# Norm and plain attention between two routed layers as one stage by groups of four tiles, and the experts' output bias split on 128 partitions

## The chip, the cores and the metric

The kernel runs on one core of a Trainium2 chip. The metric is the time of one execution in microseconds (us), the median of several runs. A core has TensorE (PE), VectorE (DVE), ScalarE (ACT), GpSimd (POOL) and SyncE (SP), which here only issues DMAs; they run side by side and wait for each other by semaphores.

## The reference

The program is a decoder of four layers over x (2 x 1024 tokens, width 256, fp32), with 77 context rows per batch element. Each layer is an attention and a feed-forward on the normed x. What this case touches:

```python
def _L2_xattn_ref(q, k, v, mask):          # q: layer norm of x; k = v = the 77 context rows
    scale = jnp.asarray(D_MODEL, q.dtype) ** (-0.5)
    logits = jnp.einsum('bqd,bkd->bqk', q, k) * scale
    logits = logits + mask.astype(q.dtype) * NEG_BIG
    weights = jax.nn.softmax(logits, axis=-1)
    return jnp.einsum('bqk,bkd->bqd', weights, v)
...
    # the feed-forward of layers 1 and 2: eight experts, with biases
    h = jax.nn.relu(jnp.einsum('td,edh->eth', x_flat, W1) + b1[:, None, :])
    expert_out = jnp.einsum('eth,ehd->etd', h, W2) + b2[:, None, :]
...
    x = x + _L1_ffn_ref(_layernorm(x, axis=-1), ...)                       # routed, two experts a token
    x = x + _L2_xattn_ref(_layernorm(x, axis=-1), ctx_1024, ctx_1024, mask_Bx1xS2_ik0)
    x = x + _L2_ffn_ref(_layernorm(x, axis=-1), ...)                       # routed by a threshold
```

Around them stand layer 0's attention and quantised feed-forward, layer 1's attention with 16 heads and self-attention with its own projections, and layer 3's attention and routed feed-forward.

## The kernel before

x lies in SBUF as 16 tiles of 128 tokens (`core.x`, in the profile `x_resid`), its norm as `x_norm`, the norm turned (width on the partitions) as `x_normT`. The program is a row of stages. In a stage each engine has its own list of instructions, in written order; at its end all engines meet, and the next stage begins on all of them. Inside a stage they wait by semaphores. All weight loads and stores go through SP's one queue, in order.

The routed layer m1 (`routed_layer`) ends by adding its rows to x in DRAM; SP then reloads x by four DMAs, a group of four tiles each. Then come:

- **the norm** (`layer_norm`, lines 136 to 222): DVE takes statistics of all 16 tiles (L177), moments (L180), adds eps (L182); ACT takes the root of all (L205), DVE its reciprocal (L184) and the 16 normed tiles (L187). PE turns four tiles at a time (L220), ACT and DVE copy one half each from PSUM to `x_normT` (L168).
- **plain attention** (`plain_cross_attention`, from L1265): PE makes the scores of all 16 tiles, two calls a tile (L1308; an fp32 call is two passes in the trace). DVE adds the mask (L1359), takes the maximum (L1362) and subtracts it (L1363) for eight tiles at a time, ACT takes the exponentials tile by tile, with their sums (L1330). When all 16 are there, PE turns them (L1316), ACT copies them (L1333), and PE multiplies by the context rows (L1324). Of each group three tiles are weighed on ACT (`shares`, L1341) and added to x on POOL (L1302), the fourth is weighed and added on DVE (L1382). DVE takes the new x's statistics and moments (L1373, L1377) and SP stores x by groups (L74).
- **the routed layer m2**, whose first steps are POOL's reciprocal roots of the moments (L1795, L1797) and DVE's normed tiles (L1982); SP fetches expert weights (L1767, L1768).

The output bias b2 of the experts (8 x 256, fp32) is added by PE in a routed tile's last matmul (L1927): it is split into three bf16 parts, on partitions 0, 32 and 64 of a tile of 65, and multiplied by `route.pick`, which is 1 on those three rows and 0 on the others. The split (`split_output_bias`, L342 to L351) is five POOL instructions over 2048 columns. For m2 it stands in the plain attention, ahead of POOL's additions to x. For m1 it stands in the self-attention, ahead of POOL's additions of `bo` (L2487).

The self-attention has a stage of projections before it (`self_attention`, first stage). There each of 16 steps makes three bf16 parts of a projection in turn on ACT (L2299, L2308) and DVE (L2344, L2352), and SP stores them by three DMAs (L2257); ACT's first part of step n waits for the stores of step n - 2, and its second part of step n - 1 comes behind it in ACT's list.

## Time and profile before

| what | value |
|---|---|
| median of 3 runs | 2260.05 us (2259.99 to 2260.06) |
| the profiled execution's own time | 2263.76 us |
| its span | 2262.0 us |
| mean granted clock of TensorE | 0.93 |
| norm stage, in the span | 1315.86 to 1331.00 us |
| plain attention's stage | 1331.00 to 1361.64 us |

The span is the time from the first to the last instruction of the profiled execution; times in the rows are from its start. "Busy" is time in which an engine ran an instruction; "idle before" is an engine's idle time ahead of it, with the engine and line that ended it. The granted clock is 1.00 for 2.4 GHz and 0.50 for 1.2 GHz. DVE instructions that follow each other overlap a little in the rows, so that the distance of their starts is busy time over their count.

### The profile page before, as it was taken

The numbers are of one execution on the slowest core, as the hardware profiler recorded it, in microseconds if no ns is written. First come the engines' busy times: TensorE is split into PE (matmuls) and PEld (weight loads), VectorE is DVE, ScalarE is ACT, GpSimd is POOL, SyncE is SP. The second block draws the span as 40 slices with busy tenths as digits, with TensorE's granted clock in tenths as the row PEclk, the third lists the DMA queues.
The fourth block names the chain that finished last, engine by engine and source line by source line (L and its number), as shares of the span: only waits on it lengthen the run. The fifth ranks groups of instructions, "written<-read, shape, count | busy, mean of one in ns | idle before, by whom it ended". The sixth has DMA issues, their size and how long they took to land. (4 is left out here: it accounts for less than half of the span.)

```text
span 2262.0 us, 39043 instructions
## 1 busy us (share of the span) xinstructions
PE 1963.4 (87%) x12250; PEld 1425.4 (63%) x12254; DVE 1058.9 (47%) x2418; ACT 911.7 (40%) x1930; POOL 758.7 (34%) x806
## 2 busy tenths in 40 slices
PE   6699989854999999849999945999999998696897
PEld 5466656522223232339999844999999997464797
DVE  6785844624877787263233245222222221486221
ACT  2322642123777777713333321333333333264132
POOL 0123963403000000043444332343443433584343
PEclk9699999976999999969999976999999999798899
DMA  4003300023111111083222129222222221205611
GB/s 160 20 1 135 113 1 1 18 81 104 37 37 49 42 37 37 2 302 104 35 32 36 29 62 357 48 35 33 36 34 35 35 33 26 69 20 185 198 34 24
DMA packets 124544, 151.27 MB, mean 67 GB/s; under 512 B 27210, under 2 KB 104875, under 8 KB 124315
## 3 DMA queue, kind: packets, MB, share of 16 engines
q1 hardware_dynamic: 93677, 117.61, 16.2%
q0 software_dynamic: 24288, 31.81, 8.7%
q10 hardware_dynamic: 6480, 0.59, 0.3%
q8 instruction: 55, 0.90, 0.2%
q14 instruction: 44, 0.36, 0.1%
HBM read 114.35 MB, written 37.36 MB: 67 GB/s over the span
## 5 line engine op out<-in xcount | busy, mean ns | idle before, releaser
L1915 PE MATMUL banks<-m_rowsT,x_normT 128*128 128x128 f32 x4032 | 481.1, 278 | 11.8 <-issue 7.6
L1915 PEld LDWEIGHTS banks<-m_rowsT,x_normT 128*128 128x128 f32 x4032 | 470.4, 195 | 29.2 <-issue 11.8
L1924 PE MATMUL banks<-m_w,m_hT 128*128 x2016 | 462.9, 383 | 7.3 <-ACT m_hT L2150 5.6
L1924 PEld LDWEIGHTS banks<-m_w,m_hT 128*128 128x128 f32 x2016 | 376.4, 192 | 57.1 <-issue 8.5
L2160 ACT ACTIVATE m_y<-banks,m_weight 128x256 f32<-128x256 f32 x126 | 59.7, 474 | 633.5 <-PE banks L1927 528.3
L2592 ACT ACTIVATE sh_pT<-banks 128x1024 f32<-128x1024 f32 x256 | 250.7, 1024 | 26.0 <-PE banks L2551 26.0
L2150 ACT ACTIVATE m_hT<-banks,m_bias 128x128 f32<-128x128 f32 x848 | 230.3, 387 | 64.5 <-PE banks L1915 60.3
L1834 POOL DMA_INDIRECT scratch_acc<-m_y,m_row_ids x106 | 169.7, 1601 | 130.8 <-ACT m_y L2160 88.5
L2616 DVE TENSOR_REDUCE sh_mhalf<-banks 128x1 f32<-128x512 f32 x308 | 194.1, 683 | 35.2 <-PE banks L2500 35.2
L2084 DVE TENSOR_SCALAR x_normT<-m_w 128x2048 f32 x129 | 158.4, 1228 | 74.7 <-issue 71.0
L1820 POOL COPY m_row_ids<-m_ids 128x1 int32 x117 | 52.0, 444 | 330.0 <-DMA scratch_acc<-m_y,m_row_ids 211.2
L2551 PE MATMUL banks<-sh_qs,sh_ks 99*128 99x512 bf16 x512 | 151.9, 381 | 10.2 <-ACT sh_pT L2592 8.0
L1823 POOL DMA_INDIRECT m_rows<-scratch_rows,m_row_ids x117 | 126.3, 1080 | 100.4 <-POOL m_row_ids L1820 98.7
L2500 PE MATMUL banks<-sh_ks,sh_qs 96*128 96x512 bf16 x410 | 135.2, 385 | 0.0
L2087 DVE TENSOR_SCALAR m_bias<-m2p_b 128x8 f32 x69 | 14.6, 212 | 255.0 <-ACT m_hT L2150 142.6
L2541 PE MATMUL banks<-sh_pT,sa_vh 128*17 128x512 f32 x1024 | 132.0, 597 | 1.2 <-ACT sh_pT L2592 1.2
L2487 POOL TENSOR_TENSOR x_norm<-x_norm,sp_bo 128x256 f32<-128x256 f32 x16 | 11.6, 726 | 338.5 <-DVE sh_m L2626 338.5
L2099 DVE COPY m_rowsT<-banks 128x256 f32<-128x256 f32 x88 | 37.4, 425 | 179.2 <-PE banks L1906 174.1
L2551 PEld LDWEIGHTS banks<-sh_qs,sh_ks 99*128 99x128 bf16 x512 | 41.1, 97 | 116.1 <-ACT sh_pT L2592 51.5
L2621 DVE CUSTOM_DVE_ANT_0 sh_rise<-banks,sh_rise 128x512 f32<-128x512 f32 x102 | 68.6, 688 | 44.2 <-ACT sh_rise L2580 43.9
L2500 PEld LDWEIGHTS banks<-sh_ks,sh_qs 96*128 96x128 bf16 x410 | 40.0, 98 | 76.8 <-DVE sh_mhalf L2616 35.9
L2580 ACT ACTIVATE sh_rise<-banks 128x512 f32<-128x512 f32 x102 | 60.2, 598 | 63.9 <-PE banks L2500 61.1
(401 smaller groups left out, 2724.9 us busy)
## 6 DMA issues: line engine op xcount, KB each, us to landing
m_w<-L_W SPq DMA_DIRECT2D x32, 1024.0 KB, 10.5
m_w<-L1f_W SPq DMA_DIRECT2D x16, 1024.0 KB, 10.1
a_bt<-bias SPq DMA_DIRECT2D x16, 616.0 KB, 3.8
scratch_parts<-sp_part SPq DMA_DIRECT2D x48, 128.0 KB, 1.9
sh_ks<-scratch_parts SPq DMA_DIRECT2D x96, 64.0 KB, 2.2
scratch_rows<-x_norm SPq DMA_DIRECT2D x12, 512.0 KB, 9.7
sh_qs<-scratch_parts SPq DMA_DIRECT2D x90, 64.0 KB, 2.3
scratch_acc<-x_resid SPq DMA_DIRECT2D x8, 512.0 KB, 3.1
```

Source lines behind the costliest of these rows:

```text
L1823: pool.indirect_dma_start(rows[:, v, :], None, table, bass.IndirectOffsetOnAxis(ap=row_ids[:, v:v + 1], axis=0), bounds_check=TOK, oob_is_ ...
L1834: pool.indirect_dma_start(stream, bass.IndirectOffsetOnAxis(ap=row_ids[:, v:v + 1], axis=0), y[:, v, :], None, bounds_check=TOK - 1, oob_i ...
L1915: mm = pe.matmul(ps[:, H_BANK[u] + f // 4, f % 4 * P:(f % 4 + 1) * P], w1_tile[:, u, k, f * P:(f + 1) * P], rowsT[:, u, k, :], start=(k == ...
L1924: mm = pe.matmul(ps[:, Y_BANK[u], 0:D], hT[:, u, f, :], w2_sb[:, bass.ds(e, 1), f, :], start=(f == 0), stop=(f == FB - 1 and not biased))
L2084: ins = dve.tensor_scalar(w1_tile[:, u, :, :], w1_sb[:, bass.ds(e, 1), :, :].rearrange("p e k f -> p (e k) f"), 0.0, None, ALU.add)
L2150: ins = act.activation(hT[:, u, f, :], ps[:, H_BANK[u] + c, j * P:(j + 1) * P], func, bias=bias[:, u, f:f + 1])
L2500: pe.matmul(ps[:, bank["a", s, c], :], qs[u][0:SR, h, t * P:(t + 1) * P], keys, start=True, stop=True).then_inc(a_mm, 1)
L2541: mm = pe.matmul(ps[32 * g:32 * g + DK + 1, O_BANK, :], vh[:, b * KT + k, head, :], pT[:, (2 * k + h) % 4, half, :], start=(k == 0), stop= ...
L2551: mm = pe.matmul(ps[:, B_BANK + 2 * (n % 2) + half, :], ks[u][:, h, k * P:(k + 1) * P], qs[u][:, h, half * CH:(half + 1) * CH], start=True ...
L2592: act.activation(pT[:, n % 4, :, :], ps[:, B_BANK + 2 * (n % 2):B_BANK + 2 * (n % 2) + 2, :], ACT.Exp, scale=DK ** -0.5).then_inc(exp_done, 1)
L2616: dve.tensor_reduce(mhalf[:, s % 2, half, col:col + 1], ps[:, bank["a", s, c], :], AX, ALU.max).then_inc(a_max, 1)
L2621: dve.tensor_tensor_reduce(more, ps[:, bank["a", s, c], :], more, 1.0, -3e38, ALU.add, ALU.max, mhalf[:, s % 2, 0, col:col + 1]).then_inc( ...
```

## The change

Three things change.

1. The norm and the plain attention are one stage. Each engine's list is written by groups of four tiles, with the groups overlapped by hand: while one group is at its scores, the next is normed. The reciprocal root is on POOL (a power of -0.5 for four tiles) instead of ACT and DVE. Both halves of `x_normT` are copied on ACT. The maximum isn't subtracted by DVE any more: its negative is the bias of ACT's exponential. Context rows and mask are fetched in the stage's first instructions, as before in the norm's.
2. The bias b2 is loaded as 128 partitions x 16 values, split into three parts there, stored to a scratch in DRAM and loaded back as 3 partitions x 2048. The routed matmul contracts three rows with a tile of ones. `route.pick` and its four memsets are gone.
3. The split for m1 moves from the self-attention's second stage to the projection stage before it, with its store behind step 6 and its load behind step 10 in SP's queue.

```diff
+            place("b2", [P, EXPERTS * D // P])
+            sb = lambda n, shape, dt: ctx.enter_context(core.nc.sbuf_tensor(f"{name}_{n}", shape, dt))
+            self.split, self.b2_parts = sb("b2_split", [P, 3, EXPERTS * D // P], BF16), sb("b2_parts", [3, EXPERTS * D], BF16)
+            self.turned = core.nc.dram_tensor(f"scratch_{name}_b2", (3, EXPERTS * D), BF16).ap()
...
-            fetch(sp, "b2", bcast(self.b2_from.rearrange("e d -> (e d)"), 65))
+            fetch(sp, "b2", self.b2_from.rearrange("e (q n) -> (e q) n", n=EXPERTS * D // P))
...
-        rest, parts = self.loads["b2"], self.b2_parts
+        rest, parts = self.loads["b2"], self.split
         self.loads.wait(pool)
-        pool.tensor_copy(parts[:], rest[:]).then_inc(split, 1)
-        pool.wait_ge(split, 1)
-        pool.tensor_tensor(rest[:], rest[:], parts[:], ALU.subtract).then_inc(split, 1)
-        pool.wait_ge(split, 2)
-        pool.tensor_copy(parts[0:33], rest[0:33]).then_inc(split, 1)
-        pool.wait_ge(split, 3)
-        pool.tensor_tensor(rest[0:1], rest[0:1], parts[0:1], ALU.subtract).then_inc(split, 1)
-        pool.wait_ge(split, 4)
-        pool.tensor_copy(parts[0:1], rest[0:1]).then_inc(split, 1)
-        pool.wait_ge(split, 5)
+        for i in range(3):
+            pool.tensor_copy(parts[:, i, :], rest[:]).then_inc(split, 1)
+            pool.wait_ge(split, 2 * i + 1)
+            if i < 2:
+                pool.tensor_tensor(rest[:], rest[:], parts[:, i, :], ALU.subtract).then_inc(split, 1)
+                pool.wait_ge(split, 2 * i + 2)
+    def store_parts(self, sp, split, moved):
+        sp.wait_ge(split, 5)
+        sp.dma_start(self.turned.rearrange("i (p n) -> p i n", p=P), self.split[:]).then_inc(moved, 16)
+    def load_parts(self, sp, moved):
+        sp.wait_ge(moved, 16)
+        sp.dma_start(self.b2_parts[:], self.turned).then_inc(moved, 16)
...
+            inputs.fetch(sp)
             params.fetch(sp)
-            inputs.wait(sp)
+            params.store_parts(sp, b2_split, b2_moved)
+            params.load_parts(sp, b2_moved)
...
+            for g in range(NCH):
+                own = slice(4 * g, 4 * g + 4)
+                pool.wait_ge(moments_done, 4 * g + 4)
+                pool.tensor_scalar(rstd[:, own], moments[:, own, 1], EPS, None, ALU.add).then_inc(eps_done, 1)
+                pool.wait_ge(eps_done, g + 1)
+                pool.tensor_tensor(rstd[:, own], rstd[:, own], half[:].broadcast_to([P, 4]), ALU.pow).then_inc(rstd_done, 1)
             params.split_output_bias(pool, b2_split)
...
+            def turn_tokens(g):
+                pe.wait_ge(normed, 4 * g + 4)
+                if g:
+                    pe.wait_ge(xT_sb, KD * g)
                 for k in range(KD):
-                    mm = pe.matmul(ps[:, t // PER, (t % PER) * KEYS:(t % PER + 1) * KEYS], core.xnT[:, k, t * P:(t + 1) * P],
-                                   core.ctxT[:, k, (t // 8) * KEYS:(t // 8 + 1) * KEYS], start=(k == 0), stop=(k == KD - 1))
-                if t % PER == PER - 1:
-                    mm.then_inc(s_mm, 1)
+                    for j in range(4):
+                        mm = pe.transpose(ps[:, T_BANKS[k], j * P:(j + 1) * P], xn[:, 4 * g + j, k * P:(k + 1) * P], core.ident[:])
+                    mm.then_inc(xT_mm, 1)
+            def scores(g):
+                pe.wait_ge(xT_sb, KD * g + KD)
+                if g:
+                    pe.wait_ge(s_ready, g)
+                for t in range(4 * g, 4 * g + 4):
+                    for k in range(KD):
+                        mm = pe.matmul(ps[:, S_BANK, t % 4 * KEYS:(t % 4 + 1) * KEYS], xnT[:, k, t * P:(t + 1) * P],
+                                       core.ctxT[:, k, t // 8 * KEYS:(t // 8 + 1) * KEYS], start=(k == 0), stop=(k == KD - 1))
+                mm.then_inc(s_mm, 1)
+            def turn_shares(g):
+                pe.wait_ge(exp_done, 4 * g + 4)
+                if g:
+                    pe.wait_ge(pT_sb, g)
+                for j in range(4):
+                    mm = pe.transpose(ps[0:KEYS, P_BANK, j * P:(j + 1) * P], p[:, 4 * g + j, :], core.ident[:])
+                mm.then_inc(pT_mm, 1)
+            def values(g):
+                pe.wait_ge(pT_sb, g + 1)
+                for j in range(4):
+                    t = 4 * g + j
+                    if g and j == 3:
+                        pe.wait_ge(y_sb, g)
+                    elif g:
+                        pe.wait_ge(share_sb, 3 * g - 2 + j)
+                    pe.matmul(ps[:, Y_BANKS[j], 0:D], pT[:, t, :], ctx_sb[:, t // 8, :], start=True, stop=True).then_inc(y_mm, 1)
+            turn_tokens(0)
+            scores(0)
+            turn_tokens(1)
+            scores(1)
+            turn_shares(0)
+            turn_tokens(2)
             inputs.wait(pe)
-            pe.wait_ge(exp_done, NT)
-            for g in range(NT // 4):
-                for j in range(4):
-                    mm = pe.transpose(ps[0:KEYS, 4 + g, j * P:(j + 1) * P], p[:, 4 * g + j, :], core.ident[:])
-                mm.then_inc(pT_mm, 1)
-            for t in range(NT):
-                pe.wait_ge(pT_sb, t // 4 + 1)
-                if t >= 4 and t % 4 == 3:
-                    pe.wait_ge(y_sb, t // 4)
-                elif t >= 4:
-                    pe.wait_ge(share_sb, 3 * (t // 4) - 2 + t % 4)
-                pe.matmul(ps[:, t % 4, 0:D], pT[:, t, :], ctx_sb[:, t // 8, :], start=True, stop=True).then_inc(y_mm, 1)
+            values(0)
+            scores(2)
+            turn_shares(1)
+            turn_tokens(3)
+            values(1)
+            scores(3)
+            turn_shares(2)
+            values(2)
+            turn_shares(3)
+            values(3)
...
+            def tokens_turned(g):
+                for k in range(KD):
+                    act.wait_ge(xT_mm, KD * g + k + 1)
+                    act.copy(xnT[:, k, g * CH:(g + 1) * CH], ps[:, T_BANKS[k], :]).then_inc(xT_sb, 1)
+            def exponentials(g):
+                act.wait_ge(below_done, g + 1)
+                for t in range(4 * g, 4 * g + 4):
+                    act.activation(p[:, t, :], s[:, t, :], ACT.Exp, bias=below[:, t:t + 1], accum_out=sums[:, t:t + 1]).then_inc(exp_done, 1)
+            def shares_turned(g):
                 act.wait_ge(pT_mm, g + 1)
-                act.copy(pT[:, 4 * g:4 * g + 4, :], ps[0:KEYS, 4 + g, :].rearrange("p (t n) -> p t n", n=P)).then_inc(pT_sb, 1)
-            act.wait_ge(rs_done, 1)
-            for g in range(NCH):
+                act.copy(pT[:, 4 * g:4 * g + 4, :], ps[0:KEYS, P_BANK, :].rearrange("p (t n) -> p t n", n=P)).then_inc(pT_sb, 1)
...
+            act.activation(warm[:], half[:], ACT.Exp)
+            tokens_turned(0)
+            tokens_turned(1)
+            exponentials(0)
+            tokens_turned(2)
+            shares_turned(0)
+            exponentials(1)
+            tokens_turned(3)
+            weighted(0)
+            shares_turned(1)
+            exponentials(2)
+            weighted(1)
+            shares_turned(2)
+            exponentials(3)
+            weighted(2)
+            shares_turned(3)
+            weighted(3)
...
+            def statistics(g):
+                dve.wait_ge(core.reloaded[g], 16 * core.reloads)
+                for t in range(4 * g, 4 * g + 4):
+                    dve.bn_stats(stats[:, t, :], x[:, t, :]).then_inc(stats_done, 1)
+                for t in range(4 * g, 4 * g + 4):
+                    dve.wait_ge(stats_done, t + 1)
+                    dve.bn_aggr(moments[:, t, :], stats[:, t, :]).then_inc(moments_done, 1)
+            def normed_tokens(g):
+                dve.wait_ge(rstd_done, g + 1)
+                for t in range(4 * g, 4 * g + 4):
+                    dve.tensor_scalar(xn[:, t, :], x[:, t, :], moments[:, t, 0:1], rstd[:, t:t + 1], ALU.subtract, ALU.mult).then_inc(normed, 1)
+            def limits(g):
+                own = slice(4 * g, 4 * g + 4)
+                dve.wait_ge(s_mm, g + 1)
+                dve.scalar_tensor_tensor(s[:, own, :], ps[:, S_BANK, 0:4 * KEYS].rearrange("p (t k) -> p t k", k=KEYS), D ** -0.5,
+                                         mf[:, g // 2, :].unsqueeze(1).broadcast_to([P, 4, KEYS]), ALU.mult, ALU.add).then_inc(s_ready, 1)
+                dve.wait_ge(s_ready, g + 1)
+                dve.tensor_reduce(mx[:, own], s[:, own, :], AX, ALU.max).then_inc(max_done, 1)
+                dve.wait_ge(max_done, g + 1)
+                dve.tensor_scalar(below[:, own], mx[:, own], -1.0, None, ALU.mult).then_inc(below_done, 1)
+            def reciprocals(g):
+                own = slice(4 * g, 4 * g + 4)
+                dve.wait_ge(exp_done, 4 * g + 4)
+                dve.reciprocal(rs[:, own], sums[:, own]).then_inc(rs_done, 1)
...
+            statistics(0)
+            statistics(1)
+            normed_tokens(0)
+            statistics(2)
+            normed_tokens(1)
+            statistics(3)
+            inputs.wait(dve)
+            dve.tensor_scalar(mf[:], mi[:], NEG, None, ALU.mult).then_inc(masked, 1)
+            dve.wait_ge(masked, 1)
+            limits(0)
+            normed_tokens(2)
+            limits(1)
+            reciprocals(0)
+            normed_tokens(3)
+            limits(2)
+            reciprocals(1)
+            outputs(0)
+            limits(3)
+            reciprocals(2)
+            outputs(1)
+            reciprocals(3)
+            outputs(2)
+            outputs(3)
...
-                    mm = pe.matmul(ps[:, Y_BANK[u], 0:D], route.pick[:], params.b2_parts[:].rearrange("p (e d) -> p e d", e=EXPERTS)[:, bass.ds(e, 1), :],
+                    mm = pe.matmul(ps[:, Y_BANK[u], 0:D], route.ones[0:3], params.b2_parts[:].rearrange("p (e d) -> p e d", e=EXPERTS)[:, bass.ds(e, 1), :],
...
+                    if n == 6:
+                        params.store_parts(sp, b2_split, b2_moved)
+                    if n == 10:
+                        params.load_parts(sp, b2_moved)
...
+                params.split_output_bias(pool, b2_split)
...
-                params.split_output_bias(pool, b2_split)
...
-                layer_norm(core, "n8", x, xn, xnT, arrivals=core.reloaded, fetch=inputs.fetch)
```

In the merged stage VectorE's list differs most. Before, in the norm and at the start of the attention (`n_` names the norm's tiles, `a_` the attention's, `banks` is PSUM):

```order
L177 BN_STATS n_stats<-x_resid 128x6 x16
L180 BN_AGGR n_moments<-n_stats 128x2 x16
L182 TENSOR_SCALAR n_moments<-n_moments 128x16
L184 RECIPROCAL n_rstd<-n_std 128x16
L187 TENSOR_SCALAR x_norm<-x_resid,n_moments,n_rstd 128x256 x16
L168 COPY x_normT<-banks 128x512 x4
```

And now, up to the scores of the first group:

```order
L1422 BN_STATS stats<-x_resid 128x6 x4
L1425 BN_AGGR moments<-stats 128x2 x4
L1422 BN_STATS stats<-x_resid 128x6 x4
L1425 BN_AGGR moments<-stats 128x2 x4
L1430 TENSOR_SCALAR x_norm<-x_resid,moments,rstd 128x256 x4
L1422 BN_STATS stats<-x_resid 128x6 x4
L1425 BN_AGGR moments<-stats 128x2 x4
L1430 TENSOR_SCALAR x_norm<-x_resid,moments,rstd 128x256 x4
L1422 BN_STATS stats<-x_resid 128x6 x4
L1425 BN_AGGR moments<-stats 128x2 x4
L1475 TENSOR_SCALAR a_mf<-a_mask 128x154
L1435 SCALAR_TENSOR_TENSOR a_s<-banks,a_mf 128x308
```

The first group is normed after eight tiles' statistics instead of 16, and statistics of later groups stand between; DVE copies no half of `x_normT`.

TensorE, before, in both stages:

```order
L220 MATMUL banks<-ident,x_norm 128x128 x32
L139 UNCONDITIONAL_BRANCH
L1304 UNCONDITIONAL_BRANCH
L1308 MATMUL banks<-ctxT_sb,x_normT 128x77 x32
L1316 MATMUL banks<-ident,a_p 77x128 x16
L1324 MATMUL banks<-a_ctx,a_pT 128x256 x16
```

and now:

```order
L1325 MATMUL banks<-ident,x_norm 128x128 x8
L1334 MATMUL banks<-ctxT_sb,x_normT 128x77 x8
L1325 MATMUL banks<-ident,x_norm 128x128 x8
L1334 MATMUL banks<-ctxT_sb,x_normT 128x77 x8
L1343 MATMUL banks<-ident,a_p 77x128 x4
L1325 MATMUL banks<-ident,x_norm 128x128 x8
L1354 MATMUL banks<-a_ctx,a_pT 128x256 x4
L1334 MATMUL banks<-ctxT_sb,x_normT 128x77 x8
L1343 MATMUL banks<-ident,a_p 77x128 x4
L1325 MATMUL banks<-ident,x_norm 128x128 x8
L1354 MATMUL banks<-a_ctx,a_pT 128x256 x4
L1334 MATMUL banks<-ctxT_sb,x_normT 128x77 x8
```

The groups' transposes, scores, transposed exponentials and values are interleaved: values of group 0 stand ahead of the scores of group 2, so that PE, which takes its list in order, waits there for ACT's copy of the exponentials.

SyncE in the projection stage, from the last load of m1's parameters (`m_b_split` is the split of b2, `scratch_parts` the stored parts), before:

```order
L127 DMA m_b_rest<-L1f_b 65x2048
L2257 DMA scratch_parts<-sp_part 128x512 x36
L2251 DMA scratch_key_steps<-sp_part_d 128x512 x3
L2257 DMA scratch_parts<-sp_part 128x512 x6
L2251 DMA scratch_key_steps<-sp_part_d 128x512 x3
```

and now:

```order
L127 DMA m1p_b<-L1f_b 128x16
L2360 DMA scratch_parts<-sp_part 128x512 x21
L348 DMA scratch_m_b<-m_b_split 128x3x16
L2360 DMA scratch_parts<-sp_part 128x512 x12
L353 DMA m_b_parts<-scratch_m_b 3x2048
L2360 DMA scratch_parts<-sp_part 128x512 x3
```

The two rows with `scratch_m_b` are new; they stand between the stores of `sp_part`, and the load of b2 is 128x16 instead of 65x2048.

## Rows read from the trace of the kernel before

**Rows 1.** Table by stage, 1315.86 to 1331.0 and 1331.0 to 1361.64, its sum.

```profile
sum 45.78, PE 24.19 PEld 21.85 DVE 31.62 ACT 17.14 POOL 22.60; mean PE 12.10 PEld 10.92 DVE 15.81 ACT 8.57 POOL 11.30
```

**Rows 2.** Timeline, norm stage: start, us, engine, line, operation, count, idle before.

```profile
1315.91 5.32 DVE L177 BATCH_NORM_STATS2 n_stats<-x_resid 128x6 f32<-128x256 f32 x16 [23.56 <-PEq L1663]
...
1321.16 1.15 DVE L180 BATCH_NORM_AGGREGATE n_moments<-n_stats 128x2 f32<-128x6 f32 x16
...
1323.09 5.26 DVE L187 TENSOR_SCALAR x_norm<-x_resid,n_moments,n_rstd 128x256 f32<-128x256 f32 x16
...
1324.52 5.12 PE L220 MATMUL banks<-ident,x_norm 128*128 128x128 f32 x32 [19.48 <-DVE x_norm L187]
```

**Rows 3.** List of waits, both stages: sum in us, times, longest.

```profile
ACT a_p L1330 <- DVE a_s L1363: 9.8, 2, 5.3
...
PE banks L1316 <- ACT a_p L1330: 8.0, 1, 8.0
```

**Rows 4.** Timeline, attention stage, DVE and POOL.

```profile
1336.79 0.80 DVE L1363 TENSOR_TENSOR a_s<-a_s,a_mx 128x616 f32<-128x616 f32 x1
...
1339.43 4.05 POOL L344 TENSOR_TENSOR m_b_rest<-m_b_rest,m_b_parts 65x2048 f32<-65x2048 f32 x1
...
1340.29 3.85 DVE L1363 TENSOR_TENSOR a_s<-a_s,a_mx 128x616 f32<-128x616 f32 x1
```

**Rows 5.** Groups of the attention stage: busy, mean ns, idle before.

```profile
L1302 POOL TENSOR_TENSOR x_resid<-x_resid,a_shares 128x256 f32<-128x256 f32 x12 | 8.3, 735 | 0.1
...
L1341 ACT ACTIVATE a_shares<-banks,a_rs 128x256 f32<-128x256 f32 x12 | 5.5, 474 | 2.0 <-PE banks L1324 1.9
...
L1330 ACT ACTIVATE a_p<-a_s 128x77 f32<-128x77 f32 x16 | 4.0, 253 | 9.8 <-DVE a_s L1363 9.8
...
L1359 DVE SCALAR_TENSOR_TENSOR a_s<-banks,a_mf 128x308 f32<-128x308 f32 x4 | 1.9, 479 | 4.5 <-PE banks L1308 4.5
```

**Rows 6.** Timeline, start of the routed stage that follows.

```profile
1361.64 0.37 SPq L1767 DMA_DIRECT2D m_w<-L_W  x1
...
1362.02 0.24 POOL L1795 TENSOR_SCALAR rstd<-moments 128x4 f32<-128x4 f32 x1 [1.72 <-POOLq L1268]
...
1362.34 1.05 POOL L1797 TENSOR_TENSOR rstd<-rstd,minus_half 128x4 f32<-128x4 f32 x1
```

**Rows 7.** Table by stretch, PE alone: us, busy (count), granted clock, DMA.

```profile
1324.50:1327.40 2.90, 2.88 (x14) 0.50 0.00 0
...
1327.40:1328.77 1.37, 1.37 (x14) 0.98 0.00 0
...
1331.00:1338.40 7.40, 7.34 (x64) 1.00 0.35 79
...
1346.40:1349.90 3.50, 3.48 (x17) 0.50 0.00 0
...
1351.20:1355.40 4.20, 4.20 (x20) 0.98 0.08 22
```

**Rows 8.** Waits of the projection stage, DMA issues, POOL in self-attention (page).

```profile
ACT sp_part L2299 <- DMA scratch_parts<-sp_part: 51.1, 14, 4.8
...
SPq L2257 <- DVE sp_part L2352: 58.0, 16, 4.8
...
scratch_parts<-sp_part SPq DMA_DIRECT2D x48, 128.0 KB, 1.9
...
scratch_rows<-x_norm ACTq DMA_DIRECT2D x3, 64.0 KB, 13.6
...
L2487 POOL TENSOR_TENSOR x_norm<-x_norm,sp_bo 128x256 f32<-128x256 f32 x16 | 11.6, 726 | 338.5 <-DVE sh_m L2626 338.5
```

**Rows 9.** Line L1927, and a weight load of 99 rows (page).

```profile
L1927 PEld LDWEIGHTS banks<-m_b_parts,route_pick x106: 97/98/98, 1030.4 to 1928.5; 65*128 65x128 bf16 x106
...
L1927 PE MATMUL banks<-m_b_parts,route_pick x106: 274/275/276, 1030.6 to 1928.7; 65*128 x106
...
L2551 PEld LDWEIGHTS banks<-sh_qs,sh_ks 99*128 99x128 bf16 x512 | 41.1, 97 | 116.1 <-ACT sh_pT L2592 51.5
```

More of the change, by code:

```diff
@@ L1326, in _ @@
+            turn_tokens(0)
[4 more added lines that the diff above has]
+            turn_tokens(2)
+            inputs.wait(pe)
+            values(0)
[8 more added lines that the diff above has]
+            values(3)
         @block.scalar
         def _(act):
-            for t in range(NT):
-                act.wait_ge(s_ready, t // 8 + 1)
-                act.activation(p[:, t, :], s[:, t, :], ACT.Exp, accum_out=sums[:, t:t + 1]).then_inc(exp_done, 1)
@@ L1331, in _ @@
-            for g in range(NT // 4):
+            def tokens_turned(g):
[6 more added lines that the diff above has]
+                    act.activation(p[:, t, :], s[:, t, :], ACT.Exp, bias=below[:, t:t + 1], accum_out=sums[:, t:t + 1]).then_inc(exp_done, 1)
@@ L1343, in _ @@
+            exponentials(1)
[9 more added lines that the diff above has]
+            weighted(3)
         @block.vector
         def _(dve):
-            count = [0]
-            def link(ins):
-                count[0] += 1
-                ins.then_inc(chain, 1)
-                dve.wait_ge(chain, count[0])
@@ L1364, in _ @@
-            dve.wait_ge(exp_done, NT)
-            dve.reciprocal(rs[:], sums[:]).then_inc(rs_done, 1)
-            dve.wait_ge(rs_done, 1)
-            def statistics(t):
+            def statistics(g):
[5 more added lines that the diff above has]
+                    dve.bn_aggr(moments[:, t, :], stats[:, t, :]).then_inc(moments_done, 1)
```

69 lines of the change are left out of this document (28 added, 41 removed).

## The prediction

> **What bounds the kernel now.** The page's shares of busy time over the whole span don't price a change to two short stages. So I read first the table by stage, for the two stretches that the change replaces: norm (from 1315.86 to 1331.0) and plain attention (on to 1361.64), together 45.78 us in which PE works 24.19 us and DVE 31.62 us [rows 1]. No engine is full there. The timeline of the norm stage shows why: DVE takes statistics of all 16 tiles (5.32 us), then all moments, then waits for one root on ACT, and PE's first transpose starts only at 1324.52, 8.6 us into the stage [rows 2]. The list of waits shows the same in the attention stage: PE stands 8.0 us until the exponentials of the last tile are there (the transposes of p wait for all 16), and ACT stands 9.8 us for DVE's subtraction of the maximum [rows 3]. The reader is to see a chain in which each step waits for all 16 tiles of the step before, on another engine.
>
> The timeline of DVE has one more thing: the subtraction on 128x616 takes 0.80 us the first time and 3.85 us the second, and the second lies beside POOL's 4.05 us subtraction for the bias split [rows 4]. The Trainium skill ("GPSIMD Engine Reference", its table of the engine) says that GpSimd and VectorE share their SBUF interfaces, with contention where a VectorE instruction has two SBUF inputs; the trace agrees, 3.05 us at this one place.
>
> **What the change does, part by part.** (1) Norm and attention become one stage of four groups of four tiles. I priced it by writing the five engines' lists in their new order and starting each instruction when its engine is free and its inputs are there, plus 0.05 us. Spacing is busy time over count: statistics 5.32/16 = 0.33, moments 1.15/16 = 0.07, normed tile 5.26/16 = 0.33 [rows 2]; a reciprocal root of four tiles on POOL 0.32 + 1.05 [rows 6]; score epilogue 0.48, join on POOL 8.3/12 = 0.69, exponential 0.25, share 0.46, PSUM copies on ACT near the share's time, 0.48 [rows 5]. A maximum over a group I take as half of the 0.80 us of eight tiles' [rows 4].
> PE depends on its clock: 14 transposes in 2.88 us at a granted 0.50 (1.2 GHz), 14 in 1.37 us at 0.98 (nearly all at 2.4 GHz); the 32 score calls are 64 passes in 7.34 us at 1.00, 0.23 a call; 20 passes of the value product take 4.20 us at 0.98, so 0.42 a call of two passes; both double at the lower level [rows 7].
> The list then runs: the stage starts at 1315.9 as now. Statistics and moments of group 0: 4 x 0.33 + 4 x 0.07 = 1.6, to 1317.5. Root 1.5 to 1319.0, covered on DVE by the statistics of group 1. Four normed tiles 1.35: 1320.4, and PE starts, 4.1 us before 1324.52. Eight transposes at the lower clock 1.7, the two ACT copies and 0.2 of handing over 0.9: 1323.0. Eight score calls of group 0, half at the lower clock, 2.4; transposes of group 1 from 1325.4, 0.9, wait for the copies 0.9, scores of group 1 1.8: 1329.0. Transposed p 0, transposes 2, 1.3, wait for three ACT copies 1.4: values 0 start at 1331.7. Values 0 and scores 2, 1.7 + 1.8; transposed p 1 and transposes 3, 1.3: 1336.5. Here is the longest hole: PE waits 2.7 us while ACT does two copies, three shares and the copy of p 1. From 1339.2: values 1, scores 3, 1.7 + 1.8, transposed p 2 and its copy 1.3, 1344.0; values 2, transposed p 3 and copy 3.0: 1347.0. Values 3 take 1.9, and the tail (DVE's last output 0.48 like the epilogue, four statistics and moments 1.6, 0.2 of landing) 2.3: 1351.3; to the next stage's first instruction 0.4, 1351.7. Now that is 1361.64 [rows 6]. Gain 9.9 us.
> The 3.05 us of DVE and one stage change lie in this sum already, since the list has neither.
> Its ends: all of PE's work at the higher clock gives 1350.3 (gain 11.3); all of it at the lower, by the same list with doubled PE times, 1367.6 (loss 6.0). PE's holes in the list are under 3 us, shorter than the 8.0 us hole of [rows 3], behind which it worked at 0.50 [rows 7]; I take most of it at the higher clock and allow 0.9 us for a stretch that is not: **gain 9.0 us**.
> (2) POOL's bias split. Its five instructions over 2048 columns (4.05 us for one [rows 4]) become five over 16 columns; small POOL instructions of this trace take 0.24 us [rows 6], so 1.2 us, after the four roots (1326.3) and before the first join (1337.8): covered tenfold. Without that cover it would be 1.2 us.
> (3) The trip through DRAM. SP gets a store and a load more in each of two stages. In the plain attention both are done before SP has anything to store (1338): nothing. In the self-attention's projection stage they stand in a queue that is on the path: ACT waits 51.1 us in 14 waits for stores of the parts to land, and each step is ACT, DVE, SP, landing, ACT [rows 8]. But SP itself stands 58.0 us in 16 waits there, 3.6 us a step, and the new DMA comes behind the step's three stores. An issue fits into that; what counts is whether 384 packets of 32 bytes are through in 3.6 us. Near rows: 128 KB of parts lands in 1.9 us, 64 KB in packets as small (2048 of them) in 13.6 us [rows 8]. Taken by packets 13.6 x 384/2048 = 2.6 us: hidden, 0 us. The far end is 13.6 - 3.6 = 10 us.
> The split leaves POOL in the self-attention itself, where it waits 338.5 us for maxima at the line that follows [rows 8]: 0 us.
> (4) The bias matmul contracts 3 rows instead of 65, 106 times. Weight load 98 ns and matmul 275 ns at 65 rows, and 97 ns for a load of 99 rows [rows 9]: rows don't show in the time, 0 us. The Trainium skill ("TensorE: Matmul & The Clock Gate", section "Step-by-step: what each phase is for") states the same, that loading time scales with columns and row count doesn't matter; were it otherwise, 106 x 0.26 us would be up to 27 us gained.
> (5) Four memsets fewer at the start and a smaller fetch: beside other loads, 0 us.
>
> **The sum.** The profiled execution took 2263.76 us for a span of 2262.0; the runs' median is 2260.05, 3.7 us below. A difference of two stages carries over: 2263.8 - 9.0 = 2254.8 for a profiled execution, 2260.05 - 9.0 = **2251.0 us** for the median, 0.40% less. What a measurement can tell from no change is about 0.2%, 4.5 us.
>
> **Rivals.**
> (a) *The holes cost more.* PE is strictly in order, and each piece of a group waits for ACT, which has copies, exponentials and shares in one queue. If PE drops to the lower clock in about half of its pieces, half of 17.3 us (1367.6 - 1350.3) goes: gain 2.7, 2257.4 us. For it: 17 transposed-p passes ran at 0.50 [rows 7], and behind short bursts. Against: scores ran at 1.00 after a stage change of 2.3 us [rows 2, 7]. The Trainium skill ("TensorE: Matmul & The Clock Gate", section "HAM oscillation — how this bites in real kernels") describes exactly this falling back between bursts. Chance 0.13.
> (b) *Slower.* PE stays at the lower clock for the whole stage: 1367.6, 2260.05 + 6.0 = 2266.1 us. It decides from 11.3/17.3 = 65% of PE's work at the lower clock. Against it: the norm's transposes rose to 0.98 after 2.9 us of work [rows 7]. Chance 0.04.
> (c) *The small packets sit in front of the part stores* in the projection stage: 10 us at most, the gain is eaten: 2261 us. It decides from 3.6 us of landing. The packet count speaks against it. Chance 0.04, and 0.02 for a dearer form with a loss.
> (d) *Nothing gained*, because the next stage waits for something that doesn't come earlier. Its first loads are issued at its own start, and POOL's roots too [rows 6]: everything there moves with it. Chance 0.03.
> (e) *More*: the bias matmul does get cheaper, up to 2224 us. Chance 0.01.
>
> **How the numbers follow.** My forecast, 2248.7 to 2255.5, has 0.73. With (a), (b), (c), (d), (e) that makes 1.00. Most of (a), 0.07, stays on the fast side of 2255.5 or at its edge; (a)'s rest 0.06, (c)'s 0.04 and (d) are within 0.2% (0.13); (b) and 0.02 of (c) slower (0.06). Faster 0.73 + 0.07 + 0.01 = 0.81. The range: from the all-higher-clock end, 2248.5, up to 2256.5, which takes in part of (a) and leaves 0.2 out.
>
> **What would show it.** In the profile after: first transpose of the merged stage 4.5 us behind its start (forecast 1320.4 against 1324.5); the stage from start to next stage's first load 36 to 37 us instead of 45.8; no DVE instruction of over 1 us in it; POOL's five split instructions under 0.3 us each, ahead of the joins; the projection stage's step still 4.9 us and its end at the same time; the bias matmul at 275 ns. The prediction is wrong if PE's clock row is near 0.5 through the stage, if ACT turns out to be the engine that everything waits for (its holes on PE over 3 us), or if the projection stage is longer.

## The result

The changed kernel takes 2287.73 us (median of 4 runs, 2282.52 to 2290.60), the kernel before 2260.06 us beside it: ratio 1.0116, 95% interval 1.0099 to 1.0133. It is 1.2% slower, where 0.4% faster was forecast: outside the range and of the other sign. The profiled execution, the slowest of the four, took 2290.6 us for a span of 2288.8, 26.8 us more span than before. The execution profiled before was 3.7 us above its own median too, so differences between the two traces needn't be those of the medians.

Where the time is, by the first instruction of each stage in the two traces (us):

```
stage                            before   after  difference
up to the projection stage        439.8   435.5    -4.3
projection stage                  101.0   100.9    -0.1
self-attention to gating (3)      434.6   434.5    -0.1
routed layer 1, with b2           340.5   351.4   +10.9
norm + plain attention             45.8    53.0    +7.2
routed layer 2, with b2           577.5   587.6   +10.1
headed attention, routed layer 3  322.8   325.8    +3.0
```

Two differences are large: both routed layers with an output bias, and the merged stage. The -4.3 and +3.0 lie in stages that the change doesn't touch; the later kernels have the same stages at either length (up to the projection stage 435.2 to 440.0 us, headed attention 124.8 to 126.9 us) whatever their edit, so I count them as spread and draw nothing from them. The second routed layer has such a spread of its own: 573.0 to 578.3 us in the seven traces whose bias matmul is over 65 rows.

**The routed layers.** The view of one line's instructions, for the bias matmul of the changed kernel, in the whole program and then in each of the two layers (duration min/median/max in ns, first and last start in us):

```profile
L2030 PEld LDWEIGHTS banks<-m_b_parts,route_ones x106: 90/91/91, 1026.5 to 1952.5; 3*128 3x128 bf16 x106
L2030 PE MATMUL banks<-m_b_parts,route_ones x106: 277/278/278, 1026.5 to 1952.6; 3*128 x106
...
  issue: 35.2, 106
...
L2030 PE MATMUL banks<-m_b_parts,route_ones x38: 277/278/278, 1026.5 to 1311.2; 3*128 x38
...
L2030 PE MATMUL banks<-m_b_parts,route_ones x68: 277/278/278, 1432.3 to 1952.6; 3*128 x68
```

The durations are near those of [rows 9], 91 for 98 ns and 278 for 275. The third row is the one to see: before this line the engine stood idle 35.2 us in 106 times, 0.33 us each, for nothing that the profile shows. The same line of before has no such row. The timeline of the weight loads shows one tile, before the change and then after it:

```profile
1600.93 3.32 PEld L1924 LDWEIGHTS banks<-m_w,m_hT 128*128 128x128 f32 x16
1604.27 0.10 PEld L1927 LDWEIGHTS banks<-m_b_parts,route_pick 65*128 65x128 bf16 x1
1604.49 3.65 PEld L1915 LDWEIGHTS banks<-m_rowsT,x_normT 128*128 128x128 f32 x32
```

```profile
1600.72 0.09 PEld L2030 LDWEIGHTS banks<-m_b_parts,route_ones 3*128 3x128 bf16 x1 [0.33 <-issue]
1600.93 3.65 PEld L2018 LDWEIGHTS banks<-m_rowsT,x_normT 128*128 128x128 f32 x32
...
1604.72 3.32 PEld L2027 LDWEIGHTS banks<-m_w,m_hT 128*128 128x128 f32 x16
1608.37 0.09 PEld L2030 LDWEIGHTS banks<-m_b_parts,route_ones 3*128 3x128 bf16 x1 [0.33 <-issue]
```

Before, the load of 65 rows starts 0.02 us behind the 16 loads of the second product (1600.93 + 3.32 = 1604.25), while their matmuls still run. After, it starts 0.33 us behind them (1608.37 against 1604.72 + 3.32 = 1608.04). Behind the small load nothing has changed: the next full load starts 0.21 us after it started (1600.93 - 1600.72), before 0.22 (1604.49 - 1604.27). From one bias matmul to the next, the pitch of the tiles, it was 7.36 us in most tiles, and is 7.65 us now (1608.37 - 1600.72). In layer 1, 38 matmuls span 284.7 us (1311.2 - 1026.5) against 274.2: +10.5 for 37 x 0.29 = 10.7. In layer 2, 67 x 0.29 would be 19.4, and the span of its 68 grew by only 10.1, to 520.3: before, PE stood 510.2 - 67 x 7.36 = 17.1 us over its pitch in this layer, now 520.3 - 67 x 7.65 = 7.8 us. A slower pitch covers stalls that were there anyway. In e1 below, at 7.36 us again, they are back: its 68 matmuls span 506.5 us, 13.4 over the pitch. What is left of them now is nearly all in one place near the layer's end, which the kernel before has too; the list of PE's waits in that stretch of the changed kernel shows it:

```profile
PE banks L2018 <- issue: 5.2, 1, 5.2
PE banks L2027 <- ACT m_hT L2253: 2.8, 1, 2.8
```

What the small stalls wait for, 0.1 to 1.2 us each before, the trace does not say in most cases.

**The merged stage.** The table by stretch of the changed kernel (us, busy and count of each engine, granted clock, DMA share, GB/s):

```profile
1322.30:1340.00 17.70, 11.62 (x52) 10.82 (x53) 12.02 (x49) 3.92 (x13) 6.26 (x13) 0.50 0.16 40
1340.00:1355.00 15.00, 11.65 (x46) 10.17 (x44) 3.76 (x13) 5.68 (x18) 0.95 (x2) 0.50 0.00 0
1355.00:1375.40 20.40, 16.38 (x48) 12.85 (x48) 9.16 (x40) 8.24 (x29) 7.63 (x11) 0.50 0.29 95
sum 53.10, PE 39.65 PEld 33.84 DVE 24.94 ACT 17.83 POOL 14.84; mean PE 13.22 PEld 11.28 DVE 8.31 ACT 5.94 POOL 4.95
```

The granted clock is 0.50, the 1.2 GHz level, from end to end, and PE's work grew from 24.19 us [rows 1] to 39.65 us. PE is busy three quarters of the stage, more than any other engine; DVE fell from 31.62 to 24.94 us. PE's timeline:

```profile
1327.03 1.97 PE L1325 MATMUL banks<-ident,x_norm 128*128 128x128 f32 x8 [15.52 <-DVE x_norm L1430]
...
1329.68 3.69 PE L1334 MATMUL banks<-ctxT_sb,x_normT 128*128 128x77 f32 x16 [0.67 <-ACT x_normT L1379]
...
1343.26 3.75 PE L1354 MATMUL banks<-a_ctx,a_pT 77*128 77x256 f32 x8 [1.25 <-ACT a_pT L1388]
1346.81 3.54 PE L1334 MATMUL banks<-ctxT_sb,x_normT 128*128 128x77 f32 x16
1350.14 1.06 PE L1343 MATMUL banks<-ident,a_p 128*77 128x128 f32 x4
1350.99 1.91 PE L1325 MATMUL banks<-ident,x_norm 128*128 128x128 f32 x8
1355.14 3.78 PE L1354 MATMUL banks<-a_ctx,a_pT 77*128 77x256 f32 x8 [2.24 <-ACT a_pT L1388]
```

The first transpose starts 4.7 us into the stage, as forecast (4.5), and the longest wait for ACT is 2.24 us (forecast 2.7). But eight score calls (16 passes) take 3.69 us, 0.46 a call, the lower clock's price. The order is the one of my list; its speed is not. And it isn't only short bursts that stay slow: from 1343.26 to 1352.90 PE works for 9.6 us without an idle time in the rows, and the clock of that stretch is 0.50.

The bias split, in the timelines of POOL and SP, is as cheap as forecast (the store of the parts has landed by the time the load is issued, 1.7 us behind it):

```profile
1332.83 0.20 POOL L339 CAST m_b_split<-m2p_b 128x16 bf16<-128x16 f32 x1
1333.11 0.21 POOL L342 TENSOR_TENSOR m2p_b<-m2p_b,m_b_split 128x16 f32<-128x16 f32 x1
...
1334.17 0.38 SPq L348 DMA_DIRECT2D scratch_m_b<-m_b_split  x1
...
1335.85 0.27 SPq L353 DMA_DIRECT2D m_b_parts<-scratch_m_b  x1
```

In the projection stage ACT's wait for the part stores is 51.0 us in 14 (was 51.1 in 14, [rows 8]):

```profile
ACT sp_part L2408 <- DMA scratch_parts<-sp_part: 51.0, 14, 4.7
```

### The profile page after: what moved, and what is told of

It reads as the page before. It is cut to its first block and busy times, and to the rows that moved or that the text cites. A ratio compares the mean times of both kernels' runs of the same rounds, so it can differ in the third digit from the quotient of the medians.

```text
span 2288.8 us, 39047 instructions
## 1 busy us (share of the span) xinstructions
PE 1999.2 (87%) x12250; PEld 1432.4 (63%) x12254; DVE 1053.7 (46%) x2419; ACT 911.3 (40%) x1932; POOL 742.4 (32%) x810
## 5 line engine op out<-in xcount | busy, mean ns | idle before, releaser
L2018 PE MATMUL banks<-m_rowsT,x_normT 128*128 128x128 f32 x4032 | 489.8, 281 | 10.3 <-issue 6.0
L2724 DVE TENSOR_REDUCE sh_mhalf<-banks 128x1 f32<-128x512 f32 x308 | 194.2, 684 | 35.2 <-PE banks L2608 35.2
L1923 POOL COPY m_row_ids<-m_ids 128x1 int32 x117 | 57.8, 494 | 333.4 <-DMA scratch_acc<-m_y,m_row_ids 208.3
L2659 PE MATMUL banks<-sh_qs,sh_ks 99*128 99x512 bf16 x512 | 151.9, 381 | 10.2 <-ACT sh_pT L2700 8.0
```

Source lines behind the costliest of these rows:

```text
L2018: mm = pe.matmul(ps[:, H_BANK[u] + f // 4, f % 4 * P:(f % 4 + 1) * P], w1_tile[:, u, k, f * P:(f + 1) * P], rowsT[:, u, k, :], start=(k == ...
L2659: mm = pe.matmul(ps[:, B_BANK + 2 * (n % 2) + half, :], ks[u][:, h, k * P:(k + 1) * P], qs[u][:, h, half * CH:(half + 1) * CH], start=True ...
L2724: dve.tensor_reduce(mhalf[:, s % 2, half, col:col + 1], ps[:, bank["a", s, c], :], AX, ALU.max).then_inc(a_max, 1)
```

## The experiments

Two causes were to be separated, each with a rival: the three rows of the bias matmul, and the clock in the merged stage. Times beside the kernel before on the same chip; an interval is that of the ratio.

### The rows of the bias matmul

The edit of e1_rows65, e3_rows32 and e4_rows64, with R = 65, 32, 64:

```diff
-self.b2_parts = sb("b2_parts", [3, EXPERTS * D], BF16)
+self.b2_parts = sb("b2_parts", [R, EXPERTS * D], BF16)
...
+        pool.memset(self.b2_parts[:], 0.0).then_inc(split, 1)
...
-        sp.dma_start(self.b2_parts[:], self.turned)
+        sp.dma_start(self.b2_parts[0:3], self.turned)
...
-pe.matmul(ps[:, Y_BANK[u], 0:D], route.ones[0:3], params.b2_parts[:]...
+pe.matmul(ps[:, Y_BANK[u], 0:D], route.ones[0:R], params.b2_parts[:]...
```

**e1_rows65.** 

> The changed kernel with one thing undone: the bias matmul contracts 65 rows again (rows 3 to 64 hold zeros, written once on POOL), from the same stationary tile of ones. Theory A (a matmul over 3 rows among matmuls over 128 does not let its weight load run ahead, about 0.29 us a tile): the tile pitch of the two routed layers with an output bias falls from 7.65 back to 7.36 us, the two layers take about 340 and 578 us instead of 351.4 and 587.6, and the time is 2287.7 - 21 = about 2267 us; the merged stage stays at 53 us. Rival B (the pitch comes from the other stationary tile, or from where the parts lie now, not from the rows): the pitch stays at 7.65 us and the time at 2288 us.

Measured: 2264.56 us, median of 10 (2262.33 to 2271.24), ratio 1.0021, 1.0010 to 1.0032. Against the changed kernel 23.2 us less by the medians, 0.95% = 21.5 us by the two ratios. The pitch is 7.36 us, layers 1 and 2 take 340.5 and 573.5 us, and the line's view has no idle time:

```profile
L2031 PEld LDWEIGHTS banks<-m_b_parts,route_ones x106: 97/98/98, 1030.5 to 1925.7; 65*128 65x128 bf16 x106
```

Theory A holds; the stationary tile and the place of the parts are as in the changed kernel, so rival B is out. A loss of 2.3 to 7.2 us is left. I put it down to the merged stage, which took 47.1 us here, not the 53 expected: only 1.3 us more than the two stages before in the traces, but 4.5 us more than the two stages of e7 below, which has the same bias part (a loss of 5.2 us by the medians).

**e2_bias_part_only.** 

> The kernel before with only the bias part of the change (split over 128 partitions, the trip through DRAM, the matmul over 3 rows); norm and plain attention stay two stages. Theory A: the first biased routed layer takes 11 us more and the second at least 10 us more, plain attention 3 us less since POOL's long subtraction is gone from beside DVE's, so 2260 + 21 - 3 = about 2278 us. Rival (the merged stage is what slows the second routed layer, by the state it leaves behind): the second biased layer stays near 577.5 us and the time is about 2268 us.

The bias part of the change as it is in the change's own diff (split, trip through DRAM, matmul over 3 rows), and only that; the line of SP in the attention stage:

```diff
             params.fetch(sp)
+            params.store_parts(sp, b2_split, b2_moved)
+            params.load_parts(sp, b2_moved)
             inputs.wait(sp)
```

Measured: 2279.54 us, median of 4, ratio 1.0089, 1.0068 to 1.0110. Layer 1 takes 350.3 us, layer 2 588.4 us with a pitch of 7.65, attention 27.2 us. The bias part alone is a loss of 19.4 us, and the rival, that the merged stage slows the layer behind it, is out.

**e3_rows32** and **e4_rows64.** 

> The changed kernel with the bias matmul over 32 rows (29 of zeros). If the number of rows counts, in proportion, the pitch lies between: 7.65 - 0.29 x 29/62 = 7.51 us. If it is a step somewhere between 32 and 65 rows, the pitch is 7.65 us as with 3; if a step lies between 3 and 32, it is 7.36 us.

> The changed kernel with the bias matmul over 64 rows (61 of zeros). If the number of rows counts in proportion, the pitch is 7.36 us as with 65. If it is a step at a half or a quarter of the array, 64 rows are on the dear side: 7.65 us.

Measured: 2284.27 and 2284.38 us (one run each), pitch 7.65 us in both, and 0.33 us idle before each load. So there is no proportion: 3, 32 and 64 rows cost the same, 65 rows nothing. In this kernel the step lies between 64 and 65.

**e8_two_bias_matmuls.** 

> The changed kernel (3 rows) with the bias matmul issued twice in a row, so that the experts' output bias is added twice. If the 0.29 us is the price of a switch from 128 to 3 rows and back, the second costs only its own 256 columns, 0.11 us: pitch 7.76 us. If each load of 3 rows has to wait until the matmul before it has ended: pitch 7.65 + 0.33 + 0.1 = about 8.0 us.

```diff
-                    mm = pe.matmul(...ones[0:3], ...b2_parts..., start=False, stop=True)
+                    for again in range(2):
+                        mm = pe.matmul(...ones[0:3], ...b2_parts..., start=False, stop=(again == 1))
```

Measured: 2291.40 us (one run). The timeline of the weight loads:

```profile
1600.19 0.11 PEld L2031 LDWEIGHTS banks<-m_b_parts,route_ones 3*128 3x128 bf16 x2 [0.33 <-issue]
1600.51 3.65 PEld L2018 LDWEIGHTS banks<-m_rowsT,x_normT 128*128 128x128 f32 x32 [0.21 <-issue]
...
1607.95 0.11 PEld L2031 LDWEIGHTS banks<-m_b_parts,route_ones 3*128 3x128 bf16 x2 [0.33 <-issue]
```

The pitch is 1607.95 - 1600.19 = 7.76 us, as forecast for a switch: two loads of 3 rows stand in one row of 0.11 us, with the one idle of 0.33 ahead of the pair and 0.21 behind it. The second low load waits for nothing, so it isn't each low load that waits, but the one that follows full-height loads. The rest of the account by a switch, that the way back has a price too, is not shown: with one low load the full load behind it starts as early as ever, and only behind the pair is there 0.21 us instead of 0.12. This kernel adds the bias twice and serves for its time alone.

### The bias part without the low matmul

**e7_bias_part_65_rows.** 

> The kernel before with the bias split on 128 partitions and the trip through DRAM, but the bias matmul over 65 rows; two stages as before. Theory: the routed layers keep the pitch of 7.36 us, the attention stage is 3 us shorter without POOL's long subtraction beside DVE's: 30.6 to 27.5 us, time 2257 us. Rival (those 3 us go to the clock phase or into the next stage): 2260 us.

The edit is e2's with R = 65. Measured: 2259.33 us, median of 10 (2255.95 to 2261.69), ratio 0.9993, 0.9981 to 1.0006. Against e2 it is 20.2 us, for the same 62 rows: the price of the low matmul a second time, in another kernel. The attention stage is 26.5 us, and the subtraction that took 3.85 us beside POOL's long instruction [rows 4] now takes 0.80 both times:

```profile
1334.12 0.80 DVE L1369 TENSOR_TENSOR a_s<-a_s,a_mx 128x616 f32<-128x616 f32 x1
...
1337.62 0.80 DVE L1369 TENSOR_TENSOR a_s<-a_s,a_mx 128x616 f32<-128x616 f32 x1
```

That stage's gain of 4.1 us shows in the trace, 3.05 of it in this one instruction; the norm ahead of it took 16.1 us against 15.1, so the two stages gain 3.2 us. The whole time doesn't settle it, since its interval (4.3 us less to 1.4 more) holds both the theory and the rival.

### The clock of the merged stage

The edit of e5_filler_at_start, on e1's kernel:

```diff
+            def fill(bank, count):
+                for _ in range(count):
+                    pe.matmul(ps[:, bank, 0:P], route.ones[:], route.ones[:], start=True, stop=True)
...
+            fill(Y_BANKS[3], 44)
             turn_tokens(0)
             scores(0)
```

and of e6_filler_at_waits in addition (the bank is always one that PE may write at that point):

```diff
             def scores(g):
-                pe.wait_ge(xT_sb, KD * g + KD)
                 if g:
                     pe.wait_ge(s_ready, g)
+                fill(S_BANK, (8, 8, 0, 0)[g])
+                pe.wait_ge(xT_sb, KD * g + KD)
...
             def values(g):
+                if g:
+                    pe.wait_ge(share_sb, 3 * g - 2)
+                fill(Y_BANKS[0], (12, 20, 16, 10)[g])
                 pe.wait_ge(pT_sb, g + 1)
```

**e5_filler_at_start.** 

> The kernel of e1_rows65 with 44 filler matmuls (128 x 128 of ones, into a PSUM bank that nobody reads then) on PE at the start of the merged stage, where PE stands 4.7 us until the first group is normed. Nothing waits for them. Theory (the stage is long because the granted clock stays at 0.50): the clock rises within the first 5 us, and if it then stays, the stage takes 37 to 38 us instead of 47.1 and the time is about 2255 us; if the waits for ACT bring it down again, about 44 us and 2261 us. Rival (the engines' order bounds the stage, not the clock): 46 to 47 us whatever the clock.

Measured: 2254.57 us, median of 10 (2248.77 to 2262.10), ratio 0.9980, 0.9963 to 0.9997; the merged stage takes 36.0 us. Against e1 (47.1 us, 2264.56) that is 11.1 us of stage and 10.0 us of time. The tables by stretch, first of e1, then of e5:

```profile
1315.80:1334.30 18.50, 12.47 (x56) 11.67 (x57) 12.83 (x53) 3.92 (x13) 8.14 (x14) 0.50 0.16 40
1334.30:1344.50 10.20, 6.62 (x46) 5.88 (x45) 3.69 (x12) 6.56 (x24) 2.05 (x3) 1.00 0.00 0
1344.50:1362.90 18.40, 14.52 (x45) 11.33 (x43) 8.41 (x37) 6.91 (x23) 6.46 (x10) 0.50 0.32 106
```

```profile
1313.70:1318.80 5.10, 5.05 (x46) 5.06 (x47) 5.05 (x22) 0.20 (x1) 2.67 (x4) 0.50 0.50 133
1318.80:1349.60 30.80, 20.87 (x144) 18.03 (x142) 21.76 (x80) 16.51 (x56) 13.88 (x22) 1.00 0.17 56
```

Without fillers the clock rises late and falls again; with 44 fillers in a stretch where PE had nothing to do, it is at 1.00 (2.4 GHz) from 5.1 us on and stays there through the waits. PE's timeline of e5 has the list of the prediction nearly as written:

```profile
1313.75 4.85 PE L1322 MATMUL banks<-route_ones 128*128 128x128 bf16 x44 [10.90 <-PEq L1772]
1318.39 1.23 PE L1330 MATMUL banks<-ident,x_norm 128*128 128x128 f32 x8
1320.35 2.01 PE L1339 MATMUL banks<-ctxT_sb,x_normT 128*128 128x77 f32 x16 [0.73 <-ACT x_normT L1385]
...
1336.79 1.99 PE L1359 MATMUL banks<-a_ctx,a_pT 77*128 77x256 f32 x8 [2.29 <-ACT a_pT L1394]
```

The rival (the order bounds the stage) is out. And the waits for ACT don't bring the clock down here: it fell in e1 at 1344.5 us, where PE had come back from a wait of 2.28 us, and it stays up in e5 through one of 2.29 us. Against the kernel before, the stage's 9.8 us (45.8 to 36.0, in the traces) are 5.1 us by the medians.

**e6_filler_at_waits** and **e10_merged_filler_again**, the same kernel on two chips. 

> As e5_filler_at_start, with fillers also ahead of PE's waits for ACT inside the stage (8, 8 before scores 0 and 1; 12, 20, 16, 10 before values 0 to 3; 6, 8 before transposing p 2 and 3), each group shorter at the higher clock than the wait it lies in. Theory: granted clock 1.0 from about 4 us into the stage to its end, stage 37 us, time about 2255 us. Rival: the fillers' own time or ACT sets the end, stage 44 us or more.

> The kernel of e6_filler_at_waits once more, on the same chip as e9_two_stages_filler, to compare the two on one chip. If the merge is worth 4 to 5 us at the higher clock, it is that much faster than e9: about 2251 us; if the clock is all, the two agree within 2 us.

Measured: 2249.15 us, median of 5, ratio 0.9946, 0.9927 to 0.9965, and 2252.56 us, median of 10 (2247.44 to 2258.17), ratio 0.9959, 0.9946 to 0.9972. The stage takes 36.6 us in both, 0.6 more than e5's. It is faster than both kernels of this study. In the traces it has no advantage over e5, whose clock stayed up without the fillers in the waits. By the medians on one chip it is 5.4 us faster than e5, but the two intervals just overlap; whether the fillers in the waits help in executions that weren't profiled is open.

**e9_two_stages_filler.** 

> The kernel of e7_bias_part_65_rows (norm and attention in two stages, 65 rows) with filler matmuls on PE: 80 at the start of the norm stage (PE waits 8.6 us there), 12 at the start of the attention stage and 100 in the wait for the exponentials. It asks how much of the gain of e5 and e6 is the merge and how much is only the clock. Theory (the merge itself is worth about 4 to 5 us once the clock is high): the two stages take 40 to 41 us against 36.0 to 36.6 of the merged one, time about 2256 us. Rival (the clock is all, the merge nothing): 36 to 38 us, time about 2252 us.

```diff
 (e7's kernel; norm stage)
+                for _ in range(80 if fillers is not None else 0):
+                    pe.matmul(core.ps[:, 7, 0:P], fillers[:], fillers[:], start=True, stop=True)
                 for g in range(NCH):
                     pe.wait_ge(tile_normed, 4 * g + 4)
 (attention stage)
+            fill(12)
             for t in range(NT):
...
+            fill(100)
             pe.wait_ge(exp_done, NT)
```

Measured: 2257.47 us, median of 10 (2249.93 to 2263.99), ratio 0.9986, 0.9972 to 0.9999. The clock is 1.00 from 4.6 us on, as in the merged kernel:

```profile
1316.20:1320.80 4.60, 4.55 (x44) 4.58 (x45) 4.55 (x14) 1.28 (x1) 0.00 (x0) 0.50 0.43 129
1320.80:1357.60 36.80, 29.33 (x295) 26.42 (x293) 24.03 (x87) 15.28 (x55) 11.06 (x18) 1.00 0.16 50
```

The two stages take 41.4 us against 36.6 merged, and e10 on the same chip is 4.9 us faster. So at the higher clock the merge itself is worth 4.8 us, and clock and merge are two effects. Without fillers the same comparison has the other sign: e1 merged 47.1 us, e7 in two stages 42.6 us, times 2264.56 and 2259.33, a loss of 5.2 us. The table of e7's two stages shows the clock that it had without a filler, 0.78 over both, where e1's stage has 0.61 (1.00 in 10.2 of 47.1 us, 0.50 in the rest):

```profile
1312.20:1328.30 16.10, 6.46 (x32) 6.23 (x32) 14.65 (x54) 3.84 (x6) 0.00 (x0) 0.55 0.13 39
1328.30:1354.80 26.50, 18.03 (x112) 16.18 (x112) 14.05 (x46) 13.03 (x49) 11.06 (x18) 0.92 0.22 68
```

## Why the prediction was wrong

- **Step (4), the bias matmul, 0 us: this is the step that failed most.** It cost 20.2 us (e2 against e7) to 23.2 us (changed kernel against e1; the profiles of these two differ in the merged stage as well). I read the durations of [rows 9], and they are right: 278 ns as forecast. But an instruction's price is its duration and the idle time ahead of it, and here that came from what stands before it: 0.33 us ahead of a low load behind full ones, 0.02 ahead of one of 65 rows. The row of 99 rows that I brought as proof lies on the harmless side of the step between 64 and 65 rows; none of the rows shown was below it. The Trainium skill ("TensorE: Matmul & The Clock Gate", section "Step-by-step: what each phase is for") says that row count doesn't matter for the loading time. That is a statement on the load, and the traces agree (91 and 98 ns); what failed is my step from the load's time to the kernel's. The only rival for this step was a gain; a loss had no place in the list, though [rows 9] bounded it from no side.
- **Step (1), the merged stage, gain 9.0 us: right in mechanism, wrong in the clock.** Start of PE 4.7 us (forecast 4.5), longest wait 2.24 us (2.7), and 36.0 us for the stage at the higher clock in e5 (forecast 36 to 37 with an allowance, 34.4 for all of it high; the exponentials, started 0.34 us apart where the list has 0.25, can account for 16 x 0.09 = 1.5 us of the difference at most).
- **The clock in step (1).** What I took for granted, "most of it at the higher clock", did not come by itself: 53.0 us in the changed kernel's profile with the clock at 0.50 throughout, where the all-lower list gave 51.7, and 47.1 in e1, e4 and e8, 44.7 in e3, with the clock high in 10 to 14 us of it. The profile of the changed kernel is rival (b), and e1's 2264.56 us lies next to (b)'s 2266.1; I gave it 0.04. The reason I gave against (b) did not carry: the norm's transposes rose to 0.98 after 2.9 us of work [rows 7], but in the changed kernel 9.6 us of work without an idle time did not raise the clock. (The reason against (a) has a misread number: the gap ahead of the scores was 1.4 us, from 1324.52 + 5.12 to 1331.06, not 2.3.) The Trainium skill ("TensorE: Matmul & The Clock Gate", section "HAM oscillation — how this bites in real kernels") describes a clock that falls back in waits for DMA between bursts, longer waits than those inside this stage. The traces agree only in part: e1's clock fell 1 us behind a wait of 2.28 us, the changed kernel's never rose to fall, and e5's stayed up through the same waits. That clock, not order, holds the stage was shown by e5. The lower clock goes with the merge in every trace without fillers (mean over norm and attention 0.76 to 0.78 in the three with two stages, 0.50 to 0.65 in the five merged ones), but why, and why one trace never rises, is open.
- **The sum.** 2260.05, + 4.4 for the merge at mostly the lower clock (e1 against before), + 23.2 for the low matmul, is 2287.7, the measured 2287.73. The parts come from differences along one line of kernels and so must add up, which proves nothing by itself. The low matmul's price taken where the merge has no part, e2 against e7, is 20.2 us; with it the sum is 2284.7. The other 3 us may be the merged stage, which in the changed kernel's profile is 5.9 us longer than in e1's. Either way the matmul is some five times the merge. One more step of my sum is not borne out: that a difference of two stages carries over from the trace before to the median. Among the later kernels it does (e5 against e1: 11.1 us of stage, 10.0 of time), against the trace before it doesn't (e5: 9.8 and 5.1); that trace is of an execution 3.7 us above the median.
- **Step (2), POOL's split, 0:** right. Five instructions of 0.20 to 0.22 us, the first join 19.9 us after the last.
- **Step (3), the DRAM trip, 0:** right. Projection stage 100.9 against 101.0 us, ACT's wait 51.0 against 51.1. Rival (c) is out.
- **Step (5):** nothing in any trace speaks against 0.
- **The 3.05 us of DVE** that lay beside POOL's subtraction were in the list rightly: e7 keeps DVE's subtraction and takes POOL's long instruction from beside it, and the second subtraction falls from 3.85 to 0.80 us, which is the contention that the Trainium skill ("GPSIMD Engine Reference", its table of the engine) names; the trace agrees.
- **Rival (d), nothing gained:** out in the form given, since a shorter stage did shorten the whole (e5 against e1). Against the kernel before, half of the stage's gain is seen in the median.

## What to carry to other kernels

A small matmul among large ones is priced by its neighbours: one over 64 rows or fewer behind matmuls over 128 cost 0.29 us each time, 106 times, though its own duration hardly changed; padding it with zero rows to 65 removed that. Look at the idle time ahead of an instruction, not only at its duration. A list of a new order needs PE's clock as much as its order: the clock read from the old pattern did not hold for the new one, and where PE idles anyway at a stage's start, a few microseconds of throwaway matmuls there decided between a loss of some 5 us and a gain of some 5.

## What the runs showed of the hardware

- The weight load of a matmul over 3, 32 or 64 rows starts 0.33 us behind the full-height loads before it; over 65 rows it follows at 0.02 us. The next full-height load follows at 0.12 us in both cases. Within a pair of low matmuls there is no idle time (e8: two for 0.11 us more).
- POOL's work on 65x2048 beside DVE's subtraction of two SBUF operands cost that instruction 3.05 us; without it both took 0.80 us.
- The exponential with a bias column (128x77) takes 355 ns against 253 without it [rows 5], in the changed kernel's groups:

```profile
L1384 ACT ACTIVATE a_p<-a_s,a_below 128x77 f32<-128x77 f32 x16 | 5.6, 355 | 0.0
```

- 44 matmuls that nobody reads took 4.85 us of idle PE time at the start of a 36 us stage, and the next 30.8 us of it ran at 1.00 with waits of up to 2.3 us in them, where the same stage without them stood at 0.50 for at least two thirds of its length in each of the five traces taken (all of 53.0 us, 36.9 of 47.1 in e1).
- 9.6 us of PE work on fp32 operands without an idle time ran at 0.50 throughout (changed kernel), where 2.9 us of transposes brought the clock up in the kernel before [rows 7]. What decides between the two no run here shows.
